# A small language-model step on one core: the first layer norm's rows turned by DMA instead of TensorE

## The chip, the core and the metric

The kernel runs on one core of one Trainium2 chip. The metric is the device time of one execution in microseconds; lower is better. The core has TensorE (PE, matmuls and transposes into PSUM), VectorE (DVE), ScalarE (ACT), GpSimd (POOL) and SyncE (SP, which issues DMAs). The engines run side by side and order themselves by semaphores; each engine executes its own instructions in the order in which they are written.

## What is computed

For 64 sequences of 256 tokens, rows of width 256:

```
h   = nan_to_num(table[ids])                       # 16384 rows of 256
x   = layernorm(h)
f,i,c = sigmoid(x Wf^T), sigmoid(x Wi^T), g(x Wh^T)   # g(z) = z + 0.5 for z >= 0, else sigmoid(z)
hid[t] = f[t]*hid[t-1] + i[t]*c[t],  hid[-1] = 0.5   # a scan along each sequence
h   = h + hid
x   = layernorm(h)
r   = relu(bitlinear(x, w_fc) + gate * x v^T fast_b^T u^T)
h   = h + bitlinear(r*r, w_proj)                   # width 1024 inside
```

The reference writes the scan in logarithms; the kernel computes the recurrence as it stands above.

## The kernel before

**Chunks and steps.** The 16384 rows are cut into 32 chunks of 512 rows (two sequences, four tiles of 128 rows). Step n (0 to 32) runs the front of chunk n (gates, scan, first residual) and the back of chunk m = n - 1 (second norm's transposes, FFN, projection, output). Steps 0 to 2 and the last ones are written out; between them a loop runs two steps per turn. All engines run the same sequence of steps, each with its own hand-written order.

**Preparing chunk c.** POOL clears `rows_raw` (L274) and gathers the rows into it (L283), three chunks ahead. DVE replaces NaN and infinities: `rows_pos` (L719), `rows_neg` (L721), and their sum `h0` (L726, `guard_sum`, in the wait for POOL's root before the second norm). `measure(0, c)` makes mean and variance (L731, L735), POOL the reciprocal root (`root`: var_eps L292, rstd L295), and `normalise(0, c)` writes `normed` (L741). PE then turns the eight 128x128 blocks of `normed` into the PSUM tensor `turned` (`turn(0, c)`, L493), ACT copies it to f16 `x_hi` (L370), and DVE subtracts, `x_lo` (L747): each f32 number goes into the matmuls as two f16 parts.

**PE's order in a step.** Six groups of eight gate matmuls (L576: w_hi and w_lo against x_hi and x_lo), with the second norm's `turn(1, m)` after the second group and the low-rank product (L550, L551) after the fourth; then the eight FFN column blocks f = 0 to 7 of five matmuls (L623, L625, L629), with `turn(0, n+1)` after f = 3; then the transposes of `hid` into the same `turned` (L645), which wait for the scans and for x_hi and x_lo of the next chunk's first norm; then 64 projection matmuls into `y_ps` (L659).

**DVE's order in a step.** measure(0, n+1); x_lo of the second norm (m); cand(0) (L912); normalise(0, n+1); scan(0) (L921); `low` (L937); the guard of chunk n+2; cand(1); scan(1); sq_hi and sq_lo (L961, L963) for p = 0, 1; x_lo of the first norm (n+1); sq_hi and sq_lo for p = 2, 3; h1 (L971); measure(1); guard_sum; normalise(1, n); y_sb (L986). Between cand and scan lies POOL's product `value` (L323).

**ACT's order in a step.** Four evictions for each half e of the gates, in the order forget, inp, cand_sig, cand_lin (L413), with the second norm's x_hi after the first inp and `low` after the second forget; then relu (L444) and square (L448) of the FFN, with the first norm's x_hi for n+1 behind the second square.

**SP** issues the loads of the weights once and one store of 512 KB per step (L254), when `out_sb` is ready (POOL, L343).

The waits ahead of the scan's transposes on PE:

```python
pe.wait_ge(scanned, 4 * (n + 1))
ahead = min(n + 2, N) if isinstance(n, int) else n + 2
pe.wait_ge(x_hi_ready[0], ahead)
pe.wait_ge(x_lo_ready[0], ahead)
```

Of the kernel before, what the change touches and what calls it, by code (L numbers as in the profile page):

```python
# [48 lines left out]
def build(nc, ids, table, wf, wi, wh, fast_b, w_fc, w_proj, u, v, gate, out):  # L49
    ctx = ExitStack()  # L50
    with ctx:
# [23 lines left out]
        rows_pos = sb("rows_pos", [P, TILES, D])  # L75
        rows_neg = sb("rows_neg", [P, TILES, D])
# [7 lines left out]
        x_hi = [sb(f"x_hi{k}", [P, KD, CHUNK], F16) for k in range(2)]  # L84
        x_lo = [sb(f"x_lo{k}", [P, KD, CHUNK], F16) for k in range(2)]
# [90 lines left out]
        pool_passed, dve_passed = sem("pool_passed"), sem("dve_passed")  # L176
# [3 lines left out]
        raw_split = sem("raw_split")  # L180
# [6 lines left out]
        x_turned = [sem("x_turned0"), sem("x_turned1")]  # L187
# [49 lines left out]
        def _(sp):  # L237
# [9 lines left out]

            def step(n, h, par):
                if isinstance(n, int) and n == 0:
                    return  # L250
# [11 lines left out]
        def _(pool):  # L262
# [86 lines left out]
        def _(act):  # L349
# [17 lines left out]
            def x_high(k, c):  # L367

                act.wait_ge(x_turned[k], c + 1)
                act.activation(x_hi[k][:, :, :], turned_cols, ACT.Copy).then_inc(x_hi_ready[k], 1)  # L370

            x_high(0, 0)
# [17 lines left out]
            def step(n, h, par):  # L390
# [3 lines left out]
                def columns():  # L394
                    wait(act, fc_done, FC * m)
                    x_high(1, m)
# [3 lines left out]
                if front:  # L400
                    for e in range(KD):
                        for q, (dst, func, bias) in enumerate((
# [17 lines left out]
                            if isinstance(n, int) and (n, e, q) == (0, 0, 1):  # L420
# [18 lines left out]
                for p in range(FC // 2):  # L439
# [20 lines left out]
        def _(pe):  # L460
# [27 lines left out]
            def turn(k, c):  # L488

                pe.wait_ge(normed_ready[k], TILES * (c + 1))  # L490
                for e in range(KD):
                    for j in range(TILES):
                        ins = pe.transpose(turned_cols[:, e, j * P:(j + 1) * P],  # L493
                                           normed[k][:, j, e * P:(e + 1) * P], ident[:, :])
                ins.then_inc(x_turned[k], 1)

            turn(0, 0)
# [42 lines left out]
            def low_rank(n, m, front):  # L540
# [8 lines left out]
                for k in range(KD):  # L549
                    pe.matmul(bank[0][:, :], low_a[:, k, :], x_hi[1][:, k, :], start=(k == 0), stop=False)  # L550
                    ins = pe.matmul(bank[0][:, :], low_a[:, k, :], x_lo[1][:, k, :], start=False, stop=(k == KD - 1))  # L551
                ins.then_inc(low_done, 1)

            def step(n, h, par):
# [3 lines left out]
                if front:  # L558
                    pe.wait_ge(x_hi_ready[0], n + 1)
                    pe.wait_ge(x_lo_ready[0], n + 1)  # L560
                    for p in range(6):
# [11 lines left out]
                        for k in range(KD):  # L573
                            for w in (w_hi, w_lo):
                                for x in (x_hi, x_lo):
                                    ins = pe.matmul(bank[gate_bank[p]][:, :], w[:, k, q, :], x[0][:, k, :],  # L576
                                                    start=(k == 0 and w is w_hi and x is x_hi),
                                                    stop=(k == KD - 1 and w is w_lo and x is x_lo))
                        ins.then_inc(gate_done, 1)
                        if back and p == 1:  # L580
                            pe.wait_ge(h1_ready, n)
                            turn(1, m)
# [11 lines left out]
                elif back:  # L594
                    pe.wait_ge(h1_ready, n)
                    turn(1, m)
                    low_rank(n, m, False)
                if isinstance(n, int) and n == 0:
                    turn(0, 1)
# [9 lines left out]
                for f in range(FC):  # L609
                    if back:  # L610
# [11 lines left out]
                        for k in range(KD):  # L622
                            pe.matmul(dst[:, :], fc_t[:, k, f * P:(f + 1) * P], x_hi[1][:, k, :],  # L623
                                      start=(k == 0), stop=False)
                            pe.matmul(dst[:, :], fc_t[:, k, f * P:(f + 1) * P], x_lo[1][:, k, :],  # L625
# [5 lines left out]
                    if f == 3 and known_below(n, N - 1) and not (isinstance(n, int) and n == 0):  # L631
                        wait(pe, x_hi_ready[1], n)
# [379 lines left out]
```

## Time and profile before

| | |
|---|---|
| median of 3 runs | 1036.16 us (1035.92 to 1037.06) |
| the profiled execution: span from first to last instruction | 1033.3 us |
| PE busy | 968.8 us, 94% |
| DVE busy | 864.6 us, 84% |
| ACT busy | 553.0 us, 54% |
| POOL busy | 489.6 us, 47% |
| HBM traffic | 19.81 MB read, 16.78 MB written |

The profile is one execution, on the same kernel as the timed runs. A busy time is the sum of an engine's instructions; matmuls overlap, so that the distance between two starts, not the duration shown, says what one costs. In a timeline row the first number is the start from the span's beginning, the second the time to the end of the last instruction of the row, and what stands in brackets is the idle time ahead of it and the instruction that ended it.

### The profile page before, as it was taken

To read this page: it belongs to the slowest core of one execution; us is meant where nothing else is said; L and a number is where in the kernel's file an instruction comes from. 1 tells how busy PE (TensorE), PEld (TensorE's weight loads), DVE (VectorE), ACT (ScalarE), POOL (GpSimd) and SP (SyncE) were. 2 spreads that over 40 slices of the span, in tenths; PEclk is the share of its full clock that TensorE was granted. 3 is DMA by queue.
4 is the path that set the end of the run, shared out by engine and by line. 5 is a ranking of instruction groups with operands and counts; after the bars stand their busy time and mean duration, and the time that the engine had idled before them with its cause. 6 is when DMAs were issued, how large, how long until landed. Compare 5 with 4: busy or idle time off the path is not lost.

```text
span 1033.3 us, 18090 instructions
## 1 busy us (share of the span) xinstructions
PE 968.8 (94%) x5825; PEld 582.6 (56%) x5825; DVE 864.6 (84%) x1570; ACT 553.0 (54%) x775; POOL 489.6 (47%) x427
## 2 busy tenths in 40 slices
PE   1779999999999999999999999999999999999987
PEld 1336655556655555665556566555656655566654
DVE  6897888888888888888888888888898888888673
ACT  3355566545556644555664455566445556545543
POOL 6525455445545544554554454555445455442210
PEclk9899999999999999999999999999999999999998
DMA  4000000000000000000000000000000000000001
GB/s 128 10 1 8 25 26 25 21 25 25 5 26 25 24 22 25 25 5 26 25 23 23 25 25 5 26 25 23 23 26 26 5 25 25 21 25 22 21 1 41
DMA packets 26582, 24.30 MB, mean 24 GB/s; under 512 B 5190, under 2 KB 25232, under 8 KB 26560
## 3 DMA queue, kind: packets, MB, share of 16 engines
q1 hardware_dynamic: 20416, 19.81, 5.8%
q0 software_dynamic: 6144, 4.21, 1.8%
q8 instruction: 12, 0.20, 0.1%
q14 instruction: 10, 0.08, 0.0%
HBM read 19.81 MB, written 16.78 MB: 35 GB/s over the span
## 4 chain that ended last, share of the span: by engine, by line
PE 44%; DVE 30%; issue 14%; POOL 6%; ACT 3%; DVEq 1%; DMA 1%; POOLq 1%; SPq 0%; ACTq 0%
PE y_ps L659 20%; PE bank L576 16%; DVE normed L741 6%; DVE hid L921 6%; DVE sq_hi L961 4%; POOL value L323 4%; DVE x_lo L747 3%; PE turned L645 3%; PE turned L493 3%; DVE cand L912 2%; DVE rows_pos L719 2%; ACT cand_lin L413 2%; DVE low L937 2%; DVE rows_neg L721 1%; POOL rstd L295 1%
## 5 line engine op out<-in xcount | busy, mean ns | idle before, releaser
L659 PE MATMUL y_ps<-proj_t,sq_hi 128*128 128x256 bf16 x1024 | 225.3, 273 | 0.0
L659 PE MATMUL y_ps<-proj_t,sq_lo 128*128 128x256 bf16 x1024 | 225.3, 273 | 0.0
L283 POOL DMA_INDIRECT rows_raw<-table,idx_now x128 | 184.8, 1444 | 58.3 <-issue 30.2
L623 PE MATMUL bank<-x_hi,fc_t 128*128 128x512 f16 x512 | 195.8, 382 | 0.7 <-issue 0.7
L625 PE MATMUL bank<-x_lo,fc_t 128*128 128x512 f16 x512 | 195.5, 382 | 0.0
L413 ACT ACTIVATE forget<-bank,w_back 128x512 f32<-128x512 f32 x64 | 44.0, 687 | 278.3 <-PE bank L576 278.3
L444 ACT ACTIVATE relu<-bank,relu_scale 128x512 f32<-128x512 f32 x256 | 164.5, 681 | 16.8 <-PE bank L629 16.8
L323 POOL TENSOR_TENSOR value<-inp,cand 128x512 f32<-128x512 f32 x64 | 81.9, 1279 | 187.2 <-DVE cand L912 187.2
L963 DVE TENSOR_TENSOR sq_lo<-sq,sq_hi 128x1024 f16<-128x1024 f32 x128 | 156.9, 1225 | 4.4
L741 DVE TENSOR_SCALAR normed<-h,moments,rstd 128x256 f32<-128x256 f32 x256 | 119.5, 529 | 43.5 <-POOL rstd L295 43.5
L576 PE MATMUL bank<-x_hi,w_hi 128*128 128x512 f16 x384 | 147.0, 383 | 2.4 <-issue 2.4
L576 PE MATMUL bank<-x_lo,w_hi 128*128 128x512 f16 x384 | 146.8, 382 | 0.0
L576 PE MATMUL bank<-x_hi,w_lo 128*128 128x512 f16 x384 | 146.6, 382 | 0.0
L576 PE MATMUL bank<-x_lo,w_lo 128*128 128x512 f16 x384 | 146.6, 382 | 0.0
L448 ACT ACTIVATE sq<-relu 128x1024 f32<-128x1024 f32 x128 | 135.4, 1058 | 4.1
L343 POOL TENSOR_TENSOR out_sb<-y_sb,h 128x1024 f32<-128x1024 f32 x32 | 75.5, 2358 | 105.2 <-DVE y_sb L986 105.2
L292 POOL TENSOR_SCALAR var_eps<-moments 128x4 f32<-128x4 f32 x64 | 38.0, 594 | 176.5 <-DVE moments L735 176.5
L921 DVE TENSOR_TENSOR_SCAN hid<-forget,value 128x256 f32<-128x256 f32 x128 | 81.1, 674 | 47.1 <-POOL value L323 47.0
L659 PEld LDWEIGHTS y_ps<-proj_t,sq_lo 128*128 128x128 f16 x1024 | 100.2, 98 | 11.8
L659 PEld LDWEIGHTS y_ps<-proj_t,sq_hi 128*128 128x128 f16 x1024 | 100.1, 98 | 11.4
L629 PE MATMUL bank<-low,low_u 128*128 128x512 f16 x256 | 97.5, 381 | 0.0
L961 DVE CAST sq_hi<-sq 128x1024 f16<-128x1024 f32 x128 | 88.7, 693 | 7.8 <-ACT sq L448 7.5
(140 smaller groups left out, 1348.1 us busy)
## 6 DMA issues: line engine op xcount, KB each, us to landing
out<-out_sb SPq DMA_DIRECT2D x32, 512.0 KB, 3.0
rows_raw<-table,idx_now POOLq DMA_INDIRECT x128, 3.0
fc_raw<-w_fc SPq DMA_DIRECT2D x1, 1024.0 KB, 7.0
pj_raw<-w_proj SPq DMA_DIRECT2D x1, 1024.0 KB, 9.1
w_raw<-wf SPq DMA_DIRECT2D x1, 256.0 KB, 3.2
w_raw<-wi SPq DMA_DIRECT2D x1, 256.0 KB, 3.5
w_raw<-wh SPq DMA_DIRECT2D x1, 256.0 KB, 4.1
ids_sb<-ids SPq DMA_DIRECT2D x1, 64.0 KB, 1.8
```

The source lines that it names most:

```text
L283: pool.indirect_dma_start(rows_raw[:, par, j, :], None, table, bass.IndirectOffsetOnAxis(ap=idx_now[:, par, j:j + 1], axis=0), bounds_chec ...
L323: pool.tensor_tensor(value[:, e, :], inp[:, e, :], cand[:, e, :], ALU.mult)\
L444: act.activation(relu[:, p % 2, f % 2, :], bank[fc_bank[f]][:, :], ACT.Relu, scale=relu_scale[:, f:f + 1]).then_inc(relu_ready, 1)
L448: act.activation(sq[:, p % 2, :, :], relu[:, p % 2, :, :], ACT.Square)\
L576: ins = pe.matmul(bank[gate_bank[p]][:, :], w[:, k, q, :], x[0][:, k, :], start=(k == 0 and w is w_hi and x is x_hi), stop=(k == KD - 1 an ...
L623: pe.matmul(dst[:, :], fc_t[:, k, f * P:(f + 1) * P], x_hi[1][:, k, :], start=(k == 0), stop=False)
L625: pe.matmul(dst[:, :], fc_t[:, k, f * P:(f + 1) * P], x_lo[1][:, k, :], start=False, stop=False)
L659: ins = pe.matmul(y_ps[:, j, :], part[:, f, j * P:(j + 1) * P], proj_t[:, f, :], start=(f == 0 and j % 2 == 0 and part is sq_hi), stop=(f ...
L741: dve.tensor_scalar(normed[k][:, j, :], rows[:, j, :], moments[k][:, j, 0:1], rstd[k][:, j:j + 1], ALU.subtract, ALU.mult).then_inc(normed ...
L921: dve.tensor_tensor_scan(hid[:, e, at], forget[:, e, at], value[:, e, at], 0.5, ALU.mult, ALU.add).then_inc(scanned, 1)
L961: dve.tensor_copy(sq_hi[:, 2 * p:2 * p + 2, :], sq[:, p % 2, :, :]).then_inc(sq_hi_ready, 1)
L963: dve.tensor_tensor(sq_lo[:, 2 * p:2 * p + 2, :], sq[:, p % 2, :, :], sq_hi[:, 2 * p:2 * p + 2, :], ALU.subtract).then_inc(sq_lo_ready, 1)
```

## The change

The first norm's normalised rows are split into two f16 parts as rows, before they are turned (`x_rows`, written by ACT and DVE), and SP turns both parts with one transposing DMA each into `x_cols`, which is double buffered; the gate matmuls read `x_cols`. PE's `turn(0, ...)` is gone, and the second norm keeps the old way. ACT's copy moves from behind the second square to behind inp of the second half, DVE's subtraction from between the squares to behind `low` (in steps 0 and 1 they stand elsewhere). L645 waits for the second norm's parts instead of the first's. The guard is two operations, the second of which reads `rows_raw` again, so that the clearing of `rows_raw` waits for `h0`.

```diff
-        rows_pos = sb("rows_pos", [P, TILES, D])
-        rows_neg = sb("rows_neg", [P, TILES, D])
+        rows_fin = sb("rows_fin", [P, TILES, D])
-        x_hi = [sb(f"x_hi{k}", [P, KD, CHUNK], F16) for k in range(2)]
-        x_lo = [sb(f"x_lo{k}", [P, KD, CHUNK], F16) for k in range(2)]
+        x_rows = sb("x_rows", [P, 2, TILES, D], F16)
+        x_cols = sb("x_cols", [P, 2, 2, TILES, KD, P], F16)
+        x_hi = sb("x_hi", [P, KD, CHUNK], F16)
+        x_lo = sb("x_lo", [P, KD, CHUNK], F16)
...
# SP
+            def turn_rows(c, par):
+                for part, ready in enumerate((x_hi_ready[0], x_lo_ready[0])):
+                    sp.wait_ge(ready, c + 1)
+                    pass_on(sp, sp_passed, c)
+                    sp.dma_start_transpose(x_cols[:, par, part, :, :, :].rearrange("p j k t -> p (j k) t"),
+                                           x_rows[:, part, :, :].rearrange("p j d -> p (j d)"))\
+                        .then_inc(x_landed, 16)
+            turn_rows(0, 0)
             def step(n, h, par):
+                if known_below(n, N - 1):
+                    wait(sp, gate_done, 6 * n)
+                    pass_on(sp, sp_passed, n)
+                    turn_rows(n + 1, 1 - par)
...
# POOL, clear(c)
-                wait(pool, raw_split, 2 * (c - 1))
+                wait(pool, h0_ready, c - 1)
...
# ACT
+            def rows_high(c):
+                act.wait_ge(normed_ready[0], TILES * (c + 1))
+                wait(act, x_landed, 32 * c)
+                act.activation(x_rows[:, 0, :, :], normed[0][:, :, :], ACT.Copy).then_inc(x_hi_ready[0], 1)
...
+                            if (e, q) == (1, 1) and known_below(n, N - 1) and not (isinstance(n, int) and n == 1):
+                                rows_high(n + 1)
...
-                    if p == 1 and known_below(n, N - 1):
-                        act.wait_ge(gate_done, 6 * (n + 1))
-                        x_high(0, n + 1)
+                    if p == 1 and isinstance(n, int) and n == 1:
+                        rows_high(n + 1)
...
# PE
-            turn(0, 0)
...
-                    pe.wait_ge(x_hi_ready[0], n + 1)
-                    pe.wait_ge(x_lo_ready[0], n + 1)
+                    pe.wait_ge(x_landed, 32 * (n + 1))
...
-                                for x in (x_hi, x_lo):
-                                    ins = pe.matmul(bank[gate_bank[p]][:, :], w[:, k, q, :], x[0][:, k, :],
+                                for part in range(2):
+                                    ins = pe.matmul(bank[gate_bank[p]][:, :], w[:, k, q, :],
+                                                    x_cols[:, par, part, :, k, :],
...
-                    if f == 3 and known_below(n, N - 1) and not (isinstance(n, int) and n == 0):
-                        wait(pe, x_hi_ready[1], n)
-                        wait(pe, x_lo_ready[1], n)
-                        turn(0, n + 1)
...
                     pe.wait_ge(scanned, 4 * (n + 1))
-                    ahead = min(n + 2, N) if isinstance(n, int) else n + 2
-                    pe.wait_ge(x_hi_ready[0], ahead)
-                    pe.wait_ge(x_lo_ready[0], ahead)
+                    wait(pe, h1_ready, n)
+                    wait(pe, x_hi_ready[1], n)
+                    wait(pe, x_lo_ready[1], n)
...
# DVE, guard and guard_sum
-                dve.tensor_scalar(rows_pos[:, :, :], rows_raw[:, par, :, :], 0.0, FMAX, ALU.max, ALU.min)\
-                    .then_inc(raw_split, 1)
-                dve.tensor_scalar(rows_neg[:, :, :], rows_raw[:, par, :, :], 0.0, -FMAX, ALU.min, ALU.max)\
-                    .then_inc(raw_split, 1)
+                dve.tensor_scalar(rows_fin[:, :, :], rows_raw[:, par, :, :], -FMAX, FMAX, ALU.max, ALU.min)\
+                    .then_inc(raw_bounded, 1)
...
-                dve.tensor_tensor(h0[:, par, :, :], rows_pos[:, :, :], rows_neg[:, :, :], ALU.add).then_inc(h0_ready, 1)
+                dve.scalar_tensor_tensor(h0[:, par, :, :], rows_raw[:, par, :, :], 0.0, rows_fin[:, :, :],
+                                         ALU.min, ALU.max).then_inc(h0_ready, 1)
...
+            def rows_low(c):
+                dve.wait_ge(x_hi_ready[0], c + 1)
+                dve.tensor_tensor(x_rows[:, 1, :, :], normed[0][:, :, :], x_rows[:, 0, :, :], ALU.subtract)\
+                    .then_inc(x_lo_ready[0], 1)
...
+                if known_below(n, N - 1) and not (isinstance(n, int) and n <= 1):
+                    rows_low(n + 1)
                 if known_below(n, N - 2):
                     guard(n + 2, 64 * (h + 2), par)
...
-                    if p == 1 and known_below(n, N - 1) and not (isinstance(n, int) and n == 0):
-                        dve.wait_ge(gate_done, 6 * (n + 1))
-                        x_low(0, n + 1)
+                    if p == 1 and first:
+                        rows_low(n + 1)
```

## Rows read from the trace of the kernel before

**Rows 1.** The page's head and part 1: busy us, share of the span, instructions.
```profile
span 1033.3 us, 18090 instructions
PE 968.8 (94%) x5825; PEld 582.6 (56%) x5825; DVE 864.6 (84%) x1570; ACT 553.0 (54%) x775; POOL 489.6 (47%) x427
```

**Rows 2.** Windows, steps 2 to 30: us, busy by engine, PE clock, DMA share.
```profile
95.13:972.22 877.09, 860.15 (x5223) 518.81 (x5221) 755.02 (x1332) 486.61 (x667) 433.39 (x367) 1.00 0.07 22
```

**Rows 3.** Timeline of PE, one step in the loop: start, length, instruction.
```profile
428.12 0.38 PE L576 MATMUL bank<-x_hi,w_hi 128*128 128x512 f16 x1
...
431.58 1.04 PE L493 MATMUL turned<-ident,normed 128*128 128x128 f32 x8
...
444.54 1.04 PE L493 MATMUL turned<-ident,normed 128*128 128x128 f32 x8
445.41 0.38 PE L623 MATMUL bank<-x_hi,fc_t 128*128 128x512 f16 x1
...
449.51 0.38 PE L629 MATMUL bank<-low,low_u 128*128 128x512 f16 x1
450.55 1.06 PE L645 MATMUL turned<-ident,hid 128*128 128x128 f32 x8 [0.66 <-DVE x_lo L747]
...
458.44 0.38 PE L576 MATMUL bank<-x_hi,w_hi 128*128 128x512 f16 x1
```

**Rows 4.** Timeline of DVE, the same step and the start of the next.
```profile
435.77 0.69 DVE L912 TENSOR_TENSOR cand<-cand_lin,cand_sig 128x512 f32<-128x512 f32 x1 [0.78 <-ACT cand_lin L413]
436.38 2.41 DVE L741 TENSOR_SCALAR normed<-h,moments,rstd 128x256 f32<-128x256 f32 x4
...
440.73 0.69 DVE L719 TENSOR_SCALAR rows_pos<-rows_raw 128x1024 f32<-128x1024 f32 x1
441.34 0.69 DVE L721 TENSOR_SCALAR rows_neg<-rows_raw 128x1024 f32<-128x1024 f32 x1
...
444.17 1.27 DVE L921 TENSOR_TENSOR_SCAN hid<-forget,value 128x256 f32<-128x256 f32 x2 [1.55 <-POOL value L323]
...
449.18 1.23 DVE L747 TENSOR_TENSOR x_lo<-turned,x_hi 128x1024 f16<-128x1024 f32 x1
...
457.20 1.19 DVE L726 TENSOR_TENSOR h<-rows_pos,rows_neg 128x1024 f32<-128x1024 f32 x1
459.64 1.38 DVE L741 TENSOR_SCALAR normed<-h,moments,rstd 128x256 f32<-128x256 f32 x4 [1.25 <-POOL rstd L295]
```

**Rows 5.** Waits over the whole span: us in total, times, longest us.
```profile
PE turned L645 <- DVE x_lo L747: 16.9, 29, 0.7
```

**Rows 6.** Timeline of ACT, then of POOL, in the same step.
```profile
438.77 0.69 ACT L413 ACTIVATE inp<-bank,w_back 128x512 f32<-128x512 f32 x1 [1.21 <-PE bank L576]
...
436.73 1.27 POOL L323 TENSOR_TENSOR value<-inp,cand 128x512 f32<-128x512 f32 x1 [1.04 <-DVE cand L912]
...
457.49 0.99 POOL L292 TENSOR_SCALAR var_eps<-moments 128x4 f32<-128x4 f32 x1 [4.30 <-DVE moments L735]
```

**Rows 7.** Groups by line and shape: busy us, mean ns, idle time before them.
```profile
L799 DVE SCALAR_TENSOR_TENSOR pj_raw<-pj_raw,pj_s,pj_a 128x1024 f32<-128x1024 f32 x2 | 2.5, 1265 | 0.0
...
L370 ACT ACTIVATE x_hi<-turned 128x1024 f16<-128x1024 f32 x64 | 65.0, 1016 | 25.7 <-PE turned L493 25.7
```

**Rows 8.** DMA: a queue's packets, MB, share; one issue's size, us to landing.
```profile
q1 hardware_dynamic: 20416, 19.81, 5.8%
...
w_raw<-wh SPq DMA_DIRECT2D x1, 256.0 KB, 4.1
```

**Rows 9.** Timelines of DVE, PE and ACT near the start, one after another.
```profile
27.13 1.23 DVE L747 TENSOR_TENSOR x_lo<-turned,x_hi 128x1024 f16<-128x1024 f32 x1 [0.65 <-ACT x_hi L370]
...
38.56 0.68 DVE L912 TENSOR_TENSOR cand<-cand_lin,cand_sig 128x512 f32<-128x512 f32 x1
...
28.45 0.59 PE L576 MATMUL bank<-x_hi,w_hi 128*128 128x512 f16 x1 [2.42 <-issue]
...
37.16 0.68 ACT L413 ACTIVATE cand_lin<-bank,w_back 128x512 f32<-128x512 f32 x1
```

More of the change, by code:

```diff
@@ L179, in build @@
         gathered = [sem("gathered_even"), sem("gathered_odd")]
[L180 removed]
+        raw_bounded = sem("raw_bounded")
         h0_ready = sem("h0_ready")
@@ L365, in _ @@
                     .then_inc(abs_summed, 1)
[L367 to L372, printed above, removed]
+            def rows_high(c):
+                act.wait_ge(normed_ready[0], TILES * (c + 1))
+                wait(act, x_landed, 32 * c)
+                act.activation(x_rows[:, 0, :, :], normed[0][:, :, :], ACT.Copy).then_inc(x_hi_ready[0], 1)
+            rows_high(0)
             def low_high(m):
@@ L395, in columns @@
                     wait(act, fc_done, FC * m)
-                    x_high(1, m)
+                    act.wait_ge(x_turned, m + 1)
+                    act.activation(x_hi[:, :, :], turned_cols, ACT.Copy).then_inc(x_hi_ready[1], 1)
                 if back and not front:
@@ L549, in low_rank @@
                 for k in range(KD):
-                    pe.matmul(bank[0][:, :], low_a[:, k, :], x_hi[1][:, k, :], start=(k == 0), stop=False)
-                    ins = pe.matmul(bank[0][:, :], low_a[:, k, :], x_lo[1][:, k, :], start=False, stop=(k == KD - 1))
+                    pe.matmul(bank[0][:, :], low_a[:, k, :], x_hi[:, k, :], start=(k == 0), stop=False)
+                    ins = pe.matmul(bank[0][:, :], low_a[:, k, :], x_lo[:, k, :], start=False, stop=(k == KD - 1))
                 ins.then_inc(low_done, 1)
@@ L574, in step @@
                             for w in (w_hi, w_lo):
-                                for x in (x_hi, x_lo):
-                                    ins = pe.matmul(bank[gate_bank[p]][:, :], w[:, k, q, :], x[0][:, k, :],
-                                                    start=(k == 0 and w is w_hi and x is x_hi),
-                                                    stop=(k == KD - 1 and w is w_lo and x is x_lo))
+                                for part in range(2):
+                                    ins = pe.matmul(bank[gate_bank[p]][:, :], w[:, k, q, :],
+                                                    x_cols[:, par, part, :, k, :],
+                                                    start=(k == 0 and w is w_hi and part == 0),
+                                                    stop=(k == KD - 1 and w is w_lo and part == 1))
                         ins.then_inc(gate_done, 1)
@@ L581, in step @@
                             pe.wait_ge(h1_ready, n)
-                            turn(1, m)
+                            turn(m)
                         if back and p == 3:
@@ L595, in step @@
                     pe.wait_ge(h1_ready, n)
-                    turn(1, m)
+                    turn(m)
                     low_rank(n, m, False)
-                if isinstance(n, int) and n == 0:
-                    turn(0, 1)
                 if isinstance(n, int) and n == 1:
@@ L622, in step @@
                         for k in range(KD):
-                            pe.matmul(dst[:, :], fc_t[:, k, f * P:(f + 1) * P], x_hi[1][:, k, :],
+                            pe.matmul(dst[:, :], fc_t[:, k, f * P:(f + 1) * P], x_hi[:, k, :],
                                       start=(k == 0), stop=False)
-                            pe.matmul(dst[:, :], fc_t[:, k, f * P:(f + 1) * P], x_lo[1][:, k, :],
+                            pe.matmul(dst[:, :], fc_t[:, k, f * P:(f + 1) * P], x_lo[:, k, :],
                                       start=False, stop=False)
@@ L738, in normalise @@
                 dve.wait_ge(rstd_ready[k], c + 1)
-                wait(dve, x_turned[k], c)
+                if k == 0:
+                    wait(dve, x_hi_ready[0], c)
+                    wait(dve, x_lo_ready[0], c)
+                else:
+                    wait(dve, x_turned, c)
                 for j in range(TILES):
@@ L882, in _ @@
             guard_sum(1, 1)
-            x_low(0, 0)
+            rows_low(0)
             def step(n, h, par):
@@ L890, in x_low_1 @@
                     wait(dve, fc_done, FC * m)
-                    x_low(1, m)
+                    dve.wait_ge(x_hi_ready[1], m + 1)
+                    dve.tensor_tensor(x_lo[:, :, :], turned_cols, x_hi[:, :, :], ALU.subtract)\
+                        .then_inc(x_lo_ready[1], 1)
                 first = isinstance(n, int) and n == 1
@@ L945, in step @@
                 if isinstance(n, int) and n == 0:
-                    x_low(0, 1)
+                    rows_low(1)
                 if first:
```

20 lines of the change are left out of this document (9 added, 11 removed).

## The prediction

> **What bounds the kernel now.** I read the page's busy times first, then one window over steps 2 to 30, then the timelines of one step by engine. TensorE (PE) is busy 94% of the span and VectorE (DVE) 84% [rows 1]; over the 29 steps from 95.13 to 972.22 us PE is busy 860.15 of 877.09 us at a granted clock of 1.00, so a step takes 30.24 us on average [rows 2], and the one I walk, from the first gate matmul at G = 428.12 to the next at 458.44, takes 30.32 [rows 3]. All times below are counted from that G.
>
> PE has one hole per step. Its last FFN matmul starts at 449.51; matmuls of this size follow each other every 0.216 us ((449.51 - 445.41)/19), so PE is free at 449.73, and the transposes of the scan's result (L645) start at 450.55: a hole of 0.82 us, ended by DVE's x_lo, which finishes at 450.41 [rows 3, 4]. The waits view has this wait 29 times [rows 5]. The x_lo in question is that of the first norm: `turn(0, n+1)` put those columns into `turned` at 444.54, and L645 needs the same PSUM. So a step is a mixed loop: gates, DVE's chain from cand(0) (G+7.65) to x_lo (G+22.29), then L645 and the projection (7.89 us, 450.55 to 458.44). DVE sees the other side: in one step it waits 0.78 us for the gates before cand(0), 1.55 for GpSimd's product before scan(1), 1.25 for the root before normalise(1) [rows 4].
>
> **Part 1: the eight first-norm transposes leave PE.** They hold PE from 444.54 to 445.41, 0.87 us, in every step whose n+1 exists [rows 3]. They lie on PE's own path: minus 0.87. With them goes their claim on `turned`: L645 now waits for the second norm's x_hi and x_lo, which are done before the FFN begins, and for the scans, which end by about 445.4 [rows 4]. Minus 0.82. PE alone would then need 30.32 - 0.87 - 0.82 = 28.63 us.
>
> **Part 2: what becomes late instead.** The projection needs sq_hi and sq_lo. Walking DVE's order with the copies moved, the last sq_lo ends near G+25.4, and PE wants it at 28.63 - 1.75 = 26.9: in time. Then h1, its statistics, the sum of the guard, GpSimd's root and normalise(1) follow, all on DVE's order; today normalise(1) starts 1.20 after the step's start (459.64 against 458.44) and ends at 2.5, and PE asks for it at 3.46 (431.58) [rows 3, 4]. That is 1 us of room, and a PE step 1.69 shorter uses it up. From there DVE's own loop sets the pace. Its two round trips through GpSimd (1.55 and 1.25) are its own and stay; the 0.78 is a wait on PE and goes. So DVE's loop now is 30.32 - 0.78 = 29.54.
>
> **Part 3: the guard.** `rows_neg` goes: 0.61 us from one start to the next (440.73, 441.34) [rows 4]. The one bounding operation that stays is a tensor_scalar like `rows_pos`. The sum becomes a scalar_tensor_tensor of the same 128x1024 f32; the kernel's own such form takes 1265 ns [rows 7] against 1.19 us for the sum [rows 4]. It is not free though it stands in the wait for the root: GpSimd's var_eps, issued beside it, takes 0.99 us, ending at 458.48, just behind the sum's 458.39 [rows 4, 6], so the root moves with it: plus 0.07. DVE's loop: 29.54 - 0.61 + 0.07 = 29.00.
>
> **Part 4: the split of the first norm on rows.** ACT's copy (x_hi, 1016 ns a piece [rows 7]) and DVE's subtraction (1.23 [rows 4]) remain, one for one, reading SBUF instead of PSUM. Both move earlier. On ACT the copy goes behind inp(1), which ends at G+11.34 [rows 6], and pushes cand_sig(1) by 0.1, where DVE, having one more operation ahead of cand(1), doesn't notice. On DVE the subtraction goes ahead of the guard: it delays cand(1) by 1.2 - 0.6, and frees as much behind; sum nothing. Its cover is thin: the copy ends at about G+12.4, DVE arrives at G+12.6; each 0.1 us that the copy is late costs 0.1. Bounds: 0 to +0.35, I take 0. One more doubtful place is normalise(0): it takes 2.41 us for four operations that take 1.38 elsewhere, because GpSimd's `value` runs beside it from 436.73 [rows 4, 6]. With DVE 0.78 earlier against GpSimd's root, one further operation may fall into that stall: 0 to +0.35, I take 0.
>
> **Part 5: the two transposing DMAs.** None is in the trace. They are issued by SP, the high part at about G+12.4, the low part at G+13.8, and the next gates wait for both: 29.0 - 12.4 = 16.6 us for D, the time from the first issue to the second landing. Lower bound: a load of 256 KB (the size of each) lands 4.1 us after its issue [rows 8], so D = 1.4 + 4.1 = 5.5. Upper bound: a packet of the hardware queue took 5.8% x 16 x 1033.3/20416 = 47 ns on one of 16 engines [rows 8]; were each DMA cut into 64-byte pieces, 4096 of them, the two would take 2 x 4096 x 0.047/16 = 24.1 us, plus 4.1: D = 28.2. In 256-byte pieces (one row of a 128-column block) it is 6.0 + 4.1 = 10. I take 6 to 10, nearest to the row of equal size: hidden, with at least 6 us to spare. On SP's queue the store of the previous chunk, ready at about G+6.3, now stands behind the waits for both parts, until G+13.8; its buffer is wanted again two steps later: nothing. DVE's normalise(0) and ACT's copy gain waits: on the previous chunk's split and landing, long past.
>
> What the row cannot show, a page says. The Trainium skill, VectorE: DVE Perf Modes, section The three transpose paths, gives 1309 ns for one 128x128 block by DMA against 390 ns on TensorE, and advises TensorE; each DMA here is eight such blocks. By an estimate from that page, sixteen in series are 20.9 us, more than the 16.6 there are, and the step would be 12.4 + 20.9 = 33.3 and the kernel slower, near 1036 + 28 x 3 = 1120 us. The Trainium skill, Advanced Engine Details and Errata, section X-Bar Transpose (TRN2), says that such DMAs are as fast as regular ones, by which the sum stays. No run here shows either.
>
> **Part 6: the ends.** At the start x_lo ended at 28.36 and gates began at 28.45 [rows 9]. With two guard operations fewer in front the low part is ready about 27.1 and lands at about 31: plus 2.7. In step 0 DVE reaches cand(0) at 38.56, without idle time, while the gates' last result was there at 37.84, so 0.7 is absorbed [rows 9]: +2.0, with 0.6 back from the guard. In step 1 PE waited for normalise before turn(0, 2) and did 0.87 of transposes: about 1.4 back. Steps 0 and 1 together: 0, between -1 and +5. Step 30 has no guard and a smaller hole: -1.1. Steps 31 and 32 don't change.
>
> **Sum.** 28 steps (2 to 29) x (30.32 - 29.00 = 1.32) = 37.0; step 30 1.1; ends 0: minus 38.1. The profiled execution has a span of 1033.3 and the median of the runs is 1036.16, 2.9 above it; the edit changes nothing outside the span. 1033.3 - 38.1 = 995.2, plus 2.9: 998.
>
> **The rivals.**
> (a) DVE's waits shrink with the rest and PE sets the pace at 28.63: 28 x 1.69 + 1.1 + 1 = 49.4, 987 us. For it: PE is the engine without holes now. Against: it needs 0.37 us a step off DVE's loop, and its round trips through GpSimd are fixed.
> (b) DVE's loop comes out longer: both doubtful places of part 4 at their bound, 29.65 us, and 5 us at the start: 28 x 0.67 + 1.1 - 5 = 14.9 saved, 1021. For it: the stalled normalise(0). Against: nothing in the sum needs more than one of them.
> (c) Slower: the DMAs are late. The next gates then start at G + 12.4 + D, and the step is that long. It decides from D = 16.6 on; at D = 17.9 the step is as long as now. At the upper bound, D = 28.2, a step is 40.6: 28 x 10.3 = +288, 1324 us. For it: nothing of the kind is in the trace, and the chain has no second buffer of rows to run ahead with. Against: plain DMAs of the size leave a factor of three (5.5 against 16.6).
> (d) The change does not shorten what it should: the gates read their moving columns from four runs of 128 instead of one of 512. Were this at half rate, 48 matmuls x 0.216 = +10.4 us a step. No row has such a read; PE's other operands of 128 columns show nothing odd.
>
> **Chances.** Forecast (990 to 1010) 0.57; (a) 0.12; (b) 0.14; (c) 0.13; (d) 0.02; something that eats the gain exactly 0.02. The range 987 to 1021 takes in the forecast, (a) and (b), and leaves out (c) and (d). A difference of 0.2% (2 us) is about what a measurement of this kernel can tell from none. Faster 0.83, within 0.02, slower 0.15.
>
> **What would show it.** Right: in the profile after, a step of 28.6 to 29.3 us; no wait of L645 on DVE; L493 with 256 instead of 512 instructions; PE's remaining wait, some 0.3 us, in front of the second norm's transposes, released by normalise(1); DVE without a wait before cand(0). Both DMAs land by G+22. Wrong: gates that wait for the landing; a DVE wait before rows_low; gate matmuls further than 0.216 us apart.

## The result, and the profile after

The changed kernel takes 1000.06 us (median of 4 runs, 998.87 to 1001.78) against 1036.32 (4 runs, 1035.92 to 1037.06) of the kernel before: a ratio of 0.9654, 95% interval 0.9638 to 0.967. The forecast of 998 and its direction held. Its profiled execution has a span of 1000.0 us, 33.3 less than before; the forecast had 38.1.

The head, the busy times, the hardware queue, the shares of the chain, and two DMA issues (size, us to landing) on the page of after:

```profile
span 1000.0 us, 17624 instructions
...
PE 942.3 (94%) x5569; PEld 554.0 (55%) x5569; DVE 844.0 (84%) x1538; ACT 553.7 (55%) x775; POOL 507.1 (51%) x427
...
q1 hardware_dynamic: 88000, 36.60, 15.1%
...
DVE 38%; issue 24%; PE 19%; POOL 13%; ACT 2%; DMA 1%; DVEq 1%; POOLq 1%; SPq 0%; ACTq 0%
...
x_cols<-x_rows SPq DMA_TRANSPOSE x64, 3.1
...
w_raw<-wh SPq DMA_DIRECT2D x1, 256.0 KB, 3.5
```

The shares of PE and DVE are those of [rows 1], so they don't say who sets the pace. The chain does: DVE and POOL hold half of it.

The timeline of PE in after, from one set of scan transposes (L658, the old L645) to the next, and the second norm's transposes (L513, the old L493) of two steps:

```profile
436.43 0.38 PE L646 MATMUL bank<-low,low_u 128*128 128x512 f16 x1
436.65 1.04 PE L658 MATMUL turned<-ident,hid 128*128 128x128 f32 x8
...
444.51 0.59 PE L594 MATMUL bank<-x_cols,w_hi 128*128 128x512 f16 x2
...
448.63 1.06 PE L513 MATMUL turned<-ident,normed 128*128 128x128 f32 x8 [0.51 <-DVE normed L758]
...
465.94 1.04 PE L658 MATMUL turned<-ident,hid 128*128 128x128 f32 x8
...
473.80 0.59 PE L594 MATMUL bank<-x_cols,w_hi 128*128 128x512 f16 x2
...
477.47 1.09 PE L513 MATMUL turned<-ident,normed 128*128 128x128 f32 x8
```

The hole of [rows 3] is closed: the scan's transposes follow the last FFN matmul after 0.22 us. The first norm's transposes are gone from PE. The gates start without a wait. What PE waits for is the normalise of the second norm: the view has a wait of 0.51 us in one step and none in the next. From the step's first gate matmul to L513 it is 4.12 us in the one (444.51 to 448.63) and 3.67 in the other (473.80 to 477.47), where before had 3.46 [rows 3], so L513 is 0.66 and 0.21 us late. Steps come in two kinds, 28.88 and 29.29 us from one L658 to the next (before: 30.20 and 30.32). What makes the two kinds differ is not shown.

DVE in after, the end of one step and the first part of the next:

```profile
451.38 1.19 DVE L910 TENSOR_TENSOR x_lo<-turned,x_hi 128x1024 f16<-128x1024 f32 x1
452.76 0.69 DVE L932 TENSOR_TENSOR cand<-cand_lin,cand_sig 128x512 f32<-128x512 f32 x1 [0.18 <-ACT cand_lin L432]
453.50 2.33 DVE L758 TENSOR_SCALAR normed<-h,moments,rstd 128x256 f32<-128x256 f32 x4
455.75 1.26 DVE L941 TENSOR_TENSOR_SCAN hid<-forget,value 128x256 f32<-128x256 f32 x2
...
457.77 1.23 DVE L764 TENSOR_TENSOR x_rows<-normed,x_rows 128x1024 f16<-128x1024 f32 x1
...
459.51 0.69 DVE L932 TENSOR_TENSOR cand<-cand_lin,cand_sig 128x512 f32<-128x512 f32 x1
461.73 1.27 DVE L941 TENSOR_TENSOR_SCAN hid<-forget,value 128x256 f32<-128x256 f32 x2 [1.53 <-POOL value L340]
...
473.59 1.19 DVE L738 SCALAR_TENSOR_TENSOR h<-rows_raw,rows_fin 128x1024 f32<-128x1024 f32 x1
476.03 1.38 DVE L758 TENSOR_SCALAR normed<-h,moments,rstd 128x256 f32<-128x256 f32 x4 [1.25 <-POOL rstd L312]
...
480.01 0.38 DVE L748 BATCH_NORM_AGGREGATE moments<-stats 128x2 f32<-128x6 f32 x4 [0.15 <-DVE stats L744]
480.31 1.22 DVE L910 TENSOR_TENSOR x_lo<-turned,x_hi 128x1024 f16<-128x1024 f32 x1
481.72 0.69 DVE L932 TENSOR_TENSOR cand<-cand_lin,cand_sig 128x512 f32<-128x512 f32 x1 [0.19 <-ACT cand_lin L432]
482.60 2.47 DVE L758 TENSOR_SCALAR normed<-h,moments,rstd 128x256 f32<-128x256 f32 x4 [0.19 <-POOL rstd L312]
484.99 1.26 DVE L941 TENSOR_TENSOR_SCAN hid<-forget,value 128x256 f32<-128x256 f32 x2
```

The wait before cand(0) went from 0.78 [rows 4] to 0.18. The two round trips through GpSimd, 1.53 and 1.25, are as they were, and nothing waits for the new subtraction's copy (L764). SP issues the first of the two transposing DMAs at 457.58, 13.07 us after the gates' first matmul; SP takes 1.24 us for one, and it lands 3.1 us after its issue. The second waits for DVE's subtraction and is issued 1.5 us after the first, so it has landed at about 444.51 + 17.7, with the next gates at 444.51 + 29.3.

**Where the 33.3 us are.** Steps 2 to 29, from the scan's transposes (L645, L658) of step 1 to those of step 29, took 847.12 us before and 813.71 after: 33.4 less. Over 28 steps that is a mean of 30.25 and of 29.06, 1.19 less in a step. Step 30 gives 1.2 more. The start costs 1.1: the first gates moved from 28.45 [rows 9] to this, where the bracket is PE's wait for the landing:

```profile
30.02 1.03 PE L594 MATMUL bank<-x_cols,w_hi 128*128 128x512 f16 x2 [16.44 <-DMA x_cols<-x_rows]
```

The last steps are 0.2 longer.

### The profile page after: what moved, and what is told of

Its sections match the earlier page's. It is cut to its first block, busy times and chain, and to the rows that moved or that the text cites. A ratio compares the mean times of both kernels' runs of the same rounds, so it can differ in the third digit from the quotient of the medians.

```text
span 1000.0 us, 17624 instructions
## 1 busy us (share of the span) xinstructions
PE 942.3 (94%) x5569; PEld 554.0 (55%) x5569; DVE 844.0 (84%) x1538; ACT 553.7 (55%) x775; POOL 507.1 (51%) x427
## 3 DMA queue, kind: packets, MB, share of 16 engines
q1 hardware_dynamic: 88000, 36.60, 15.1%
## 4 chain that ended last, share of the span: by engine, by line
DVE 38%; issue 24%; PE 19%; POOL 13%; ACT 2%; DMA 1%; DVEq 1%; POOLq 1%; SPq 0%; ACTq 0%
PE bank L594 8%; DVE normed L758 7%; DVE sq_hi L983 7%; DVE hid L941 5%; POOL rstd L312 4%; DVE stats L744 4%; POOL value L340 4%; PE y_ps L672 3%; DVE h L992 3%; POOL var_eps L309 3%; DVE cand L932 3%; POOL out_sb L360 2%; PE turned L513 2%; DVE rows_fin L732 2%; PE bank L640 2%
## 5 line engine op out<-in xcount | busy, mean ns | idle before, releaser
L594 PE MATMUL bank<-x_cols,w_hi 128*128 128x512 f16 x768 | 230.3, 382 | 16.4 <-DMA x_cols<-x_rows 16.4
L594 PE MATMUL bank<-x_cols,w_lo 128*128 128x512 f16 x768 | 230.3, 382 | 0.0
L300 POOL DMA_INDIRECT rows_raw<-table,idx_now x128 | 200.6, 1567 | 58.3 <-issue 30.2
L594 PEld LDWEIGHTS bank<-x_cols,w_hi 128*128 128x128 f16 x768 | 75.3, 98 | 94.4 <-DMA x_cols<-x_rows 16.8
L594 PEld LDWEIGHTS bank<-x_cols,w_lo 128*128 128x128 f16 x768 | 75.6, 98 | 91.9 <-issue 2.2
L309 POOL TENSOR_SCALAR var_eps<-moments 128x4 f32<-128x4 f32 x64 | 38.1, 595 | 125.9 <-DVE moments L748 125.9
L646 PE MATMUL bank<-low,low_u 128*128 128x512 f16 x256 | 98.2, 384 | 0.0
```

Source lines behind the costliest of these rows:

```text
L300: pool.indirect_dma_start(rows_raw[:, par, j, :], None, table, bass.IndirectOffsetOnAxis(ap=idx_now[:, par, j:j + 1], axis=0), bounds_chec ...
L594: ins = pe.matmul(bank[gate_bank[p]][:, :], w[:, k, q, :], x_cols[:, par, part, :, k, :], start=(k == 0 and w is w_hi and part == 0), stop ...
```

## The experiments

Theory: after is paced by DVE's loop through GpSimd (29.0), PE's own loop is 28.6, the guard counts where DVE is the late one, and the DMAs are hidden with some 11 us of room. Rivals: PE paces; the DMAs are nearly late; the gain comes from PE's 0.87 us alone. Each kernel's median is given with its ratio to the kernel before, run on the same chip.

### The parts, each alone

**e1**: the kernel before, with the new guard only.

```diff
-dve.tensor_scalar(rows_pos[:, :, :], rows_raw[:, par, :, :], 0.0, FMAX, ALU.max, ALU.min)
-dve.tensor_scalar(rows_neg[:, :, :], rows_raw[:, par, :, :], 0.0, -FMAX, ALU.min, ALU.max)
+dve.tensor_scalar(rows_fin[:, :, :], rows_raw[:, par, :, :], -FMAX, FMAX, ALU.max, ALU.min)
...
-dve.tensor_tensor(h0[:, par, :, :], rows_pos[:, :, :], rows_neg[:, :, :], ALU.add)
+dve.scalar_tensor_tensor(h0[:, par, :, :], rows_raw[:, par, :, :], 0.0, rows_fin[:, :, :], ALU.min, ALU.max)
```

> The kernel before with the two-operation guard alone; the rows are still turned on TensorE. My theory: in the kernel before a step is a mixed loop in which DVE's chain from cand(0) to x_lo, the guard in it, decides when PE may start the scan's transposes. One DVE operation less (0.61 us) shrinks PE's hole of 0.82 us to about 0.2: 28 steps x 0.61 = 17 us, 1019 us. Rival: PE's own 94% sets the pace and the guard lies beside it: 1036 us.

Measured: 1030.49 us, ratio 0.9952 (0.9935 to 0.9969). A miss: 5 us instead of 17. DVE between the guard and cand(1) in e1, and PE's hole:

```profile
438.70 0.69 DVE L718 TENSOR_SCALAR rows_fin<-rows_raw 128x1024 f32<-128x1024 f32 x1
439.78 0.69 DVE L911 TENSOR_TENSOR cand<-cand_lin,cand_sig 128x512 f32<-128x512 f32 x1 [0.38 <-ACT cand_lin L412]
...
448.39 1.06 PE L644 MATMUL turned<-ident,hid 128*128 128x128 f32 x8 [0.53 <-DVE x_lo L746]
```

The operation is gone, and cand(1) now waits 0.38 us for ACT's last gate: before, 0.61 of guard covered that wait. The steps became 0.12 shorter.

**e2**: after, with the old guard (the diff of e1 turned round).

> The changed kernel with the old three-operation guard; the rows are turned by DMA. My theory: DVE sets the pace now, so the operation put back costs its whole 0.61 us a step: 28 x 0.61 = 17 us, 1017 us. Rival: PE sets the pace (28.63 us of its own) and has waits to give back: then only what exceeds them shows, 0 to 0.2 us a step, 1000 to 1005 us.

Measured: 1018.34 us, ratio 0.9849 (0.9823 to 0.9876), as expected. Steps 29.48 and 29.89, each 0.60 longer than after. PE in e2:

```profile
456.18 1.06 PE L514 MATMUL turned<-ident,normed 128*128 128x128 f32 x8 [1.10 <-DVE normed L759]
```

PE's wait for normalise(1) is 1.10 instead of 0.51. In the other kind of step PE now waits too, 0.67 us. So the guard alone is worth 5 us, the turning alone 17 (1035.3, the kernel before in this set of runs, to 1018.3), both together 36: they don't add up. With the subtraction of 1.14 us ahead of cand(1), DVE is the late one there, and the guard's 0.6 counts in full.

### Who paces after

**e4**: after, with eight transposes on PE whose result nobody uses, behind the fourth FFN block, without a wait: the 0.87 us that the change took away, added back.

```diff
+if f == 3 and known_below(n, N - 1) and not (isinstance(n, int) and n <= 1):
+    for e in range(KD):
+        for j in range(TILES):
+            pe.transpose(turned_cols[:, e, j * P:(j + 1) * P], fc_raw[:, j, e * P:(e + 1) * P], ident[:, :])
```

> The changed kernel with eight idle transposes put back on PE after f = 3, of a tensor that never changes, with no wait (their result is overwritten by the scan's transposes). My theory: PE's own loop grows by 0.87 from 28.63 to 29.50 us, DVE's is 29.08, so a step grows by 0.42: +12 us, 1012 us. Rivals: PE sets the pace today: +0.87 a step, 1024 us; PE has more room than I count: 1000 us.

Measured: 1014.03 us, ratio 0.9802 (0.9783 to 0.9821). All steps are 29.46 or 29.47, the two kinds gone, and PE waits for nothing in them: PE's own loop is 29.47 - 0.87 = 28.60 us, and of the 0.87 only 29.47 - 29.06 = 0.41 showed. PE alone does not pace after, and its 0.87 us alone are less than the 1.19 that a step lost.

**e3**: after, with the second of the two gate products on DVE, which saves its round trip of 1.53 us to GpSimd.

```diff
-for e in range(KD):        # GpSimd
+for e in (0,):             # GpSimd
...
+if e in (1,):              # DVE, behind cand(e)
+    dve.wait_ge(cand_ready, 2 * n + e + 1)
+    wait(dve, scanned, 4 * (n - 1) + 2 * e + 2)
+    dve.tensor_tensor(value[:, e, :], inp[:, e, :], cand[:, e, :], ALU.mult).then_inc(value_ready, 1)
```

> The changed kernel with the gate product of the second half computed on DVE instead of GpSimd. My theory: the step is as long as DVE's order with its round trips. From cand(1) to scan(1) it takes 2.22 us through GpSimd and would take about 1.3 on DVE alone, so DVE's loop falls by 0.9, below PE's own 28.63, and PE sets the pace: 28 x (29.08 - 28.63) = 12 us, 988 us. Rival: DVE is bound by its busy time; one operation of 0.6 to 0.7 us more per step makes it slower: 28 x 0.6 = 17 us, 1017 us.

Measured: 1006.30 us, ratio 0.9722 (0.9705 to 0.9738): slower than after, where the theory had 988. Most steps are 29.15 or 29.47. The scan had no wait any more, but normalise(0) had grown. In e3, DVE's normalise(0) in two steps, what GpSimd does in another, PE's wait for `low`, which DVE writes behind normalise(0) and scan(0), and the normalise's group (busy, mean ns of one, idle before):

```profile
453.36 3.04 DVE L758 TENSOR_SCALAR normed<-h,moments,rstd 128x256 f32<-128x256 f32 x4
...
482.61 3.34 DVE L758 TENSOR_SCALAR normed<-h,moments,rstd 128x256 f32<-128x256 f32 x4 [0.19 <-POOL rstd L312]
...
424.15 1.27 POOL L340 TENSOR_TENSOR value<-inp,cand 128x512 f32<-128x512 f32 x1 [0.29 <-DVE cand L932]
425.36 0.95 POOL L291 MEMSET rows_raw<- 128x1024 f32 x1
...
487.92 0.39 PE L646 MATMUL bank<-low,low_u 128*128 128x512 f16 x1 [0.71 <-DVE low L962]
...
L758 DVE TENSOR_SCALAR normed<-h,moments,rstd 128x256 f32<-128x256 f32 x256 | 142.6, 618 | 47.9 <-POOL rstd L312 47.2
```

On GpSimd's order the clearing of the next rows stood behind the second product. With that product gone it runs right behind the first one, beside normalise(0), whose four operations take 3.04 and 3.34 us (in most other steps 3.2) instead of 2.33 and 2.47. PE, which waited for normalise(1) in after, now waits for `low`.

**e8**: e3, and GpSimd holds the clearing back until the second product is done.

```diff
+pool.wait_ge(value_ready, 2 * n + 2)
 clear(n + 3, 1 - par)
```

> The changed kernel with the second gate product on DVE, and GpSimd's clearing of the gathered rows held back until that product is done, so that it doesn't run beside DVE's normalise(0). My theory: the round trip of 2.22 us becomes 1.5 and normalise(0) goes back from 3.0 to 3.3 us to 2.3; DVE's loop falls to about 28.4 and PE's own 28.63 sets the pace: 28 x 0.45 = 12 us, 988 us. Rival: what made the kernel without the hold slow is the additional work of DVE, not GpSimd beside it: 1004 to 1006 us again.

Measured: 990.30 us (986.56 to 990.98), ratio 0.9567 (0.9551 to 0.9582). Steps 28.60 and 28.64. In e8 normalise(0) is back to what it was (2.34, and 2.48 in the other kind of step):

```profile
445.79 2.34 DVE L759 TENSOR_SCALAR normed<-h,moments,rstd 128x256 f32<-128x256 f32 x4
```

One wait on GpSimd turned 1006 into 990. It holds back the clearing and the gather behind it; of these the clearing (and an index copy of 0.2 us) stood beside normalise(0) in e3, while the gather began only as normalise(0) ended. From cand(1) to scan(1) DVE takes 1.54 us now instead of 2.22, and the steps stop at PE's 28.60.

**e9**: e8 with both products on DVE (`for e in ()` on GpSimd, `if e in (0, 1)` on DVE).

> Both gate products on DVE, GpSimd's clearing held back as before. Then nothing runs beside normalise(0), which should take 1.4 us instead of 2.3; DVE's loop is near 28.2. My theory: PE sets the pace at 28.63 as with one product moved: 988 us; if PE's own loop is what I count, this one is not faster than the other by more than 2 us. Rival: the pace is still DVE's and GpSimd's, then it is faster by up to 0.3 us a step, 980 us, or slower by DVE's 0.8 us of added work, 1000 us.

Measured: 985.77 us (985.51 to 986.44), ratio 0.9522 (0.9506 to 0.9538): the fastest of all, faster than both kernels. In e9 DVE's product and normalise(0), the busy times, and PE's two sets of transposes:

```profile
445.39 0.69 DVE L938 TENSOR_TENSOR value<-inp,cand 128x512 f32<-128x512 f32 x1
446.00 1.38 DVE L759 TENSOR_SCALAR normed<-h,moments,rstd 128x256 f32<-128x256 f32 x4
...
PE 934.6 (95%) x5569; PEld 553.4 (56%) x5569; DVE 858.8 (87%) x1602; ACT 553.3 (56%) x775; POOL 434.8 (44%) x363
...
429.10 1.04 PE L659 MATMUL turned<-ident,hid 128*128 128x128 f32 x8
...
440.44 1.06 PE L514 MATMUL turned<-ident,normed 128*128 128x128 f32 x8
...
457.74 1.04 PE L659 MATMUL turned<-ident,hid 128*128 128x128 f32 x8
```

With nothing of GpSimd's beside it, normalise(0) takes 1.38. DVE is busier than in after (858.8 against 844.0), and the kernel is faster. PE waits for nothing in the step, and the steps are those of e8 (28.59 and 28.64), so 28.6 is PE's own loop. The spans of the two profiles, 984.5 and 984.0, are alike too. Where the 4 us between the medians lie is open: e8's profiled execution was the fastest of its four (986.56), and of the others there is no profile.

**e10**: e9 with the old guard, to see what the guard is worth where PE paces.

> The kernel with rows turned by DMA and both gate products on DVE, with the old three-operation guard. If PE sets the pace there (28.62 us a step in every step), DVE's waits of 0.19 (cand(0)) and 0.17 to 0.29 us (sq_hi) take up most of the 0.61 us put back: 0 to 0.2 us a step, 986 to 991 us. Rival: DVE is again as late as PE and the operation costs its whole 0.61, 1003 us.

Measured: 990.09 us (989.28 to 991.04), ratio 0.9567 (0.9551 to 0.9583). Steps 28.59 and 28.68: the guard's 0.6 us on DVE show as at most 0.04 in a step, 0.6 us over steps 2 to 29. The rest of the 3 us by which the span is longer than e9's lies outside them, 2.7 of it ahead of step 2.

### The transposing DMAs

**e5** and **e6**: after, with 2 or 6 more transposing DMAs per step, each issued when the one before has landed; the gates wait for the last.

```diff
+for extra in range(2):     # e6: range(6), and 128 for 64
+    sp.wait_ge(x_landed, 64 * c + 32 + 16 * extra)
+    ...
+    sp.dma_start_transpose(x_cols[:, par, 1, :, :, :]..., x_rows[:, 1, :, :]...).then_inc(x_landed, 16)
```

> The changed kernel, where SP turns the low part two more times into the same place, each time after the landing before, and the gates wait for all. The high part is issued at 13.1 us after the start of the step's gates and the low part has landed at about 17.6; the next gates start at 29.1. My theory: the landing has about 11.5 us of room, each further transposing DMA takes 3.1 (issue to landing), 6.2 in all: the steps stay at 29.08 us, and only the start, where the gates wait for the DMAs, gets longer: 1006 to 1010 us. Rival: the DMAs get in the way of other work (ports, queues) even where nobody waits for them: more than 0.2 us a step, over 1012 us.

Measured: 1012.05 us, ratio 0.9773 (0.9757 to 0.9789). The steps are 28.87 and 29.29, those of after. The time is that of the rival (over 1012), its mechanism is not: all of the 11.5 us of span are at the start, where the gates wait for the landing, more than the 6 to 10 expected. So the landing has 6.6 us of room at least (two more DMAs of 3.30, by e6), and twice as many of them slow nothing in a step.

> The same with six more: 17.6 + 6 x 3.1 = 36.2 us after the start of the gates. My theory: here the landing sets the pace, as in the slower rival of the prediction; a step takes about 36.2 to 36.5 us, 28 x 7.2 = +202 and some 35 at the start: 1235 us, and PE waits for the DMA before the gates. Rival: a DMA on an otherwise idle queue is quicker than its 3.1, say 2: 29.6 us a step, 1030 us.

Measured: 1336.85 us, ratio 1.2911 (1.2886 to 1.2937): late, as both theories had it, but by 100 us more than expected. Steps 3 to 29 take 37.9 to 41, 39.0 on average. SP's issues and PE's first gates in e6, and windows of PE behind that wait (from:to, width, then busy (count) of PE, PEld, DVE, ACT and POOL, the granted clock, the DMAs' share, GB/s):

```profile
475.54 17.73 SPq L261 DMA_TRANSPOSE x_cols<-x_rows  x6
...
455.81 1.03 PE L600 MATMUL bank<-x_cols,w_hi 128*128 128x512 f16 x2 [8.10 <-DMA x_cols<-x_rows]
...
455.80:459.00 3.20, 3.19 (x8) 1.19 (x9) 0.00 (x0) 0.00 (x0) 0.38 (x1) 0.50 0.49 164
459.00:462.00 3.00, 3.00 (x10) 1.13 (x9) 0.00 (x0) 0.69 (x1) 0.00 (x0) 0.62 0.00 0
462.00:470.00 8.00, 8.00 (x43) 4.10 (x42) 5.17 (x8) 5.10 (x8) 1.26 (x1) 1.00 0.00 0
```

Six serial DMAs cost 3.30 us each, their issue included. The surplus is the clock: after 8.10 us of waiting PE's granted clock is 0.50 (the level of 1.2 GHz), so the gates run at half speed, ACT and DVE get them late, and the next chunk's rows are split at G + 15.1 instead of 13.1. 15.1 + 4.6 + 6 x 3.3 = 39.5 against 39.0 measured. A late DMA thus costs its lateness and a slow start behind it.

### What made the hole

**e11**: the kernel before, with the second product on DVE and the hold of e8. If DVE's chain ahead of x_lo makes PE's hole of 0.82, the hole must shrink.

> The kernel before (rows turned on TensorE, three-operation guard) with the second gate product on DVE and GpSimd's clearing held back. After the run with the guard alone my theory is amended: DVE's chain enters the step of the kernel before at cand(1), which ACT's eviction of the last gates holds to about 0.2 us behind DVE, so work ahead of cand(1) is worth 0.15 a step at most, work behind it counts in full. The round trip of 2.23 us becomes 1.5: x_lo is 0.7 us earlier and PE's hole of 0.82 closes to about 0.1: 28 x 0.7 = 20 us, 1015 us. Rival: the kernel before is bound by PE's own work and the hole is filled by another wait: 1031 to 1036 us.

Measured: 1022.35 us, ratio 0.9872 (0.9856 to 0.9888); steps 29.75, 0.5 less, not 0.7. DVE, ACT and PE in e11:

```profile
442.10 0.69 DVE L967 CAST sq_hi<-sq 128x1024 f16<-128x1024 f32 x1
...
444.08 1.23 DVE L748 TENSOR_TENSOR x_lo<-turned,x_hi 128x1024 f16<-128x1024 f32 x1
...
441.00 1.06 ACT L449 ACTIVATE sq<-relu 128x1024 f32<-128x1024 f32 x1
...
444.98 0.38 PE L630 MATMUL bank<-low,low_u 128*128 128x512 f16 x1
445.45 1.06 PE L646 MATMUL turned<-ident,hid 128*128 128x128 f32 x8
```

x_lo ends at 445.31 and L646 starts at 445.45: still tied to each other. PE's hole is 445.45 - 444.98 - 0.22 = 0.25 us, where it was 0.82, and in the other kind of step 0.26, where it was 0.71. That is 0.57 and 0.45, and the steps are shorter by just this (30.32 to 29.75, 30.20 to 29.76): the hole was what x_lo's lateness cost. From cand(1) to scan(1) DVE saves 0.68 us (1.55 instead of 2.23). Some of it is lost ahead of x_lo, where the second sq_hi starts at 442.10, as ACT's square ends (442.06): from the first sq_hi to the second it takes 1.96 us in one kind of step and 2.07 in the other, where before had 1.85 and 1.84. That is 0.11 and 0.23, which leaves 0.57 and 0.45.

## Why the prediction held, point by point

The lengths of steps, from one L658 (or its like) to the next, in us:

| kernel | the two kinds | what differs |
|---|---|---|
| before | 30.20, 30.32 | |
| e1 | 30.09, 30.19 | before, new guard |
| e11 | 29.75, 29.76 | before, second product on DVE, hold |
| e2 | 29.48, 29.89 | after, old guard |
| e4 | 29.46, 29.47 | after, 0.87 us more on PE |
| e3 | 29.15, 29.47 (most) | after, second product on DVE |
| after | 28.88, 29.29 | |
| e5 | 28.87, 29.29 | after, 2 more DMAs |
| e10 | 28.59, 28.68 | e9, old guard |
| e8, e9 | 28.60, 28.64; 28.59, 28.64 | after, 1 or 2 products on DVE, hold |

**Part 1, PE.** Right, and closely: PE's loop was to be 28.63; it is 28.60 by e4 and by e8. The hole of 0.82 and the 0.87 are both gone.

**Part 2, what is late next.** Right: normalise(1) is what PE waits for, and DVE's loop sets the pace. L513 is late by 0.66 and 0.21 us, 0.44 on average, and the steps are longer than e8's by 29.06 - 28.63 = 0.43 on average, so what holds L513 is all that holds the step (the forecast had 29.00 - 28.63 = 0.37). "The 0.78 goes" was too good: 0.18 of the wait stays. I took it as a wait on PE alone. It is a mixed loop (normalise(1), PE's transposes, the last gates, ACT, cand(0)) as against DVE's own work in the meantime. When both shrink, the wait ends where the two are equal, not at zero. And 0.78 was one of two kinds of steps. In before's other kind DVE reads so:

```profile
463.62 0.38 DVE L735 BATCH_NORM_AGGREGATE moments<-stats 128x2 f32<-128x6 f32 x4 [0.15 <-DVE stats L731]
464.16 1.22 DVE L747 TENSOR_TENSOR x_lo<-turned,x_hi 128x1024 f16<-128x1024 f32 x1 [0.16 <-ACT x_hi L370]
465.99 0.69 DVE L912 TENSOR_TENSOR cand<-cand_lin,cand_sig 128x512 f32<-128x512 f32 x1 [0.61 <-ACT cand_lin L413]
```

**Part 3, the guard.** The 0.61 is right in after (e2: +0.60). It would have been wrong for the kernel before (e1: 0.12) and for e9 (0.04 at most): an operation is worth its time only where its engine is the late one at the next meeting point. The added 0.07 was nothing: the scalar_tensor_tensor with a constant takes what the sum took, 1.19 us. Its row in after's groups:

```profile
L738 DVE SCALAR_TENSOR_TENSOR h<-rows_raw,rows_fin 128x1024 f32<-128x1024 f32 x32 | 38.3, 1196 | 0.1
```

**Part 4, the split on rows.** The copy was in time (0, as taken). The second doubtful place did cost: from cand(0) to scan(0) DVE took 2.94 us before (435.77 to 438.71 on the timeline of [rows 4]), and takes 2.99 in one kind of step after (452.76 to 455.75) and 3.27 in the other (481.72 to 484.99). The stalled normalise itself stayed as it was (2.33 and 2.47, before 2.41), so it is not the further stalled operation I had in mind: normalise(0) starts later behind cand(0), by 0.1 to 0.3 us. In the second kind the bracket names what it waits for, GpSimd's root (0.19).

Walking DVE from start to start, as the mean of the two kinds, gives the whole step:

| stretch of DVE's order | before | after | change | predicted |
|---|---|---|---|---|
| x_lo to cand(0): the wait for the last gates | 1.92 | 1.40 | -0.52 | -0.78 |
| moments to x_lo: the wait for the copy x_hi | 0.50 | 0.30 | -0.20 | none |
| cand(0) to scan(0): the wait for the root | 2.94 | 3.13 | +0.19 | 0 (to 0.35) |
| low to cand(1), and the squares: guard, subtraction | 9.95 | 9.29 | -0.66 | -0.61 |
| the sum of the guard | 1.19 | 1.19 | 0 | +0.07 |
| together | | | -1.19 | -1.32 |

The fourth row is 1.21 and 8.74 before (440.73 to 441.94, 445.36 to 454.10), 1.74 and 7.55 after. The second row is a wait that I had not seen, since the step I walked has it as a gap of 0.08 without a bracket, and the other kind as 0.16.

**Part 5, the DMAs.** Hidden, as taken, and rival (c) is dead for this kernel: D is 1.5 + 3.1 = 4.6 us in one kind of step and 1.9 + 3.1 = 5.0 in the other, below my lower bound of 5.5. That was no lower bound: 4.1 us is the slowest of three loads of 256 KB on before's page, whose others landed in 3.2 and 3.5, and a DMA here landed in 3.1. The mechanism of rival (c) is real, as e6 shows. Its point of decision (16.6 for D) was about right: after has 29.1 - 13.1 = 16.0. Its price was too low, since the sum lacked the clock. The trace also decides between the two pages' estimates. A transposing DMA of eight blocks lands in 3.1 us, where a plain load of 256 KB needs 3.0 to 3.5 in after. This agrees with the Trainium skill, Advanced Engine Details and Errata, X-Bar Transpose (TRN2). My estimate of 1120 us fell: it took the 1309 ns that the Trainium skill, VectorE: DVE Perf Modes, The three transpose paths, gives for one block times the blocks of a DMA, 10.5 us for eight, and the page doesn't say that blocks in one DMA add up so.

**Part 6, the start.** Taken 0, measured +1.1, within -1 to +5.

**The sum.** 28 steps were to give 37.0 and gave 33.4. Of the 3.6 missing, 1.9 is that I walked the longer of two kinds of steps (28 x (30.32 - 30.25)) and 1.7 that after's mean is 29.06 and not 29.00. The span shrank by 33.3 where 38.1 was forecast. The medians shrank by 36.3: the profiled execution of after, at 1001.78, was the slowest of its four, and stands 1.7 above its median.

Two things in the closeness are luck. The terms missed more than their sum did: by the table the wait for the gates gave 0.26 less than taken and the root cost 0.19 that was taken at 0, while the wait for x_hi gave 0.20 that I had not counted and two smaller terms came out 0.12 better; 0.13 is left. And the 2.9 us added for the median, which before's span lacks, has no match in after, where the span of the profiled execution (1000.0) and the median (1000.06) are alike. So a span that missed by 4.8 us became a median that missed by 2.

**Rival (a)**, PE sets the pace at 28.63, was one product and one wait away: e8 and e9 are that case, and their 990.3 and 985.8 stand about its 987. "Its round trips through GpSimd are fixed" was true of the change, not of the kernel. **Rival (d)** is dead: the gates' matmuls are 0.215 us apart (two in 0.43, 444.51 and 444.94 on the timeline), though they read four runs of 128.

## What to carry to other kernels

Ask of each operation removed which engine is late at the next meeting point: the same 0.61 us of VectorE was worth 0.60, 0.12 and at most 0.04 per step in three kernels that differ only in what stands beside it. Walk every kind of step before multiplying by the number of steps, since steps can alternate, and treat a wait as the difference of two paths, which shrinks to what is left between them. And when work leaves a helper engine, look at what moves up behind it there: in e3 a clearing nobody waited for fell beside the critical operation and ate the gain, and one wait gave it back.

## What the runs showed of the hardware

**GpSimd beside VectorE.** The same four operations took 1.38 us alone (e9), 2.33 and 2.47 beside GpSimd's product (after; e8 has 2.34 and 2.48), and 3.04 and 3.34 beside its product and clearing (e3). The normalise's mean over the whole of e9 and e3, against 530 ns in after:

```profile
L759 DVE TENSOR_SCALAR normed<-h,moments,rstd 128x256 f32<-128x256 f32 x256 | 90.1, 416 | 45.2 <-POOL rstd L312 45.2
```

It is 416 ns in e9 and 618 in e3. That the two engines share their SBUF interfaces is what the Trainium skill says (GPSIMD Engine Reference, Specifications); the trace agrees in that the two slow each other, and puts the price at up to 2.4 times an operation's time. The bound of 0.35 that I set on one further stalled operation was too low for what e3 then showed (0.7 and 0.9 on top of after's 2.33 and 2.47).

**A transposing DMA.** 256 KB of f16 from SBUF to SBUF costs SP 1.24 us of issue, where a store of 512 KB costs 0.38, and lands 3.1 us after its issue. It is cut into pieces of about 256 bytes: the queue has 88000 packets against 20416 [rows 8], 67584 / 64 = 1056 for each DMA. With twice as many of them (e5) the steps are as long as in after, 28.87 and 29.29.

**The clock.** After PE had waited 8.10 us (e6) its granted clock was 0.50 for the next 3.2 us and 0.62 on average in the 3 behind. In after, with waits of 0.51 us, it is 1.00 over steps 2 to 29.
